# Adaptive-layernorm transformer block on eight cores: modulation vectors computed ahead of the layernorm, and the second gate folded into the down-projection weights

## What is computed

```python
mod = silu(c) @ wmod                         # [1, 6*2048] per core
sa, ca, ga, sb, cb, gb = split(mod, 6)
ga = (2*(ga >= 0) - 1) * maximum(abs(ga), 0.25)
gb = (2*(gb >= 0) - 1) * maximum(abs(gb), 0.25)
h = layernorm(x) * (1 + ca) + sa
x = x + ga * (attention(h, w_qkv) @ w_out)   # 16 heads of 128, no mask
h = layernorm(x) * (1 + cb) + sb
# router: silu(h @ r1.T) @ r2.T, the 16 best of 64 blocks of 128 hidden units
hidden = silu(h @ gate_w.T) * (h @ up_w.T) * block_mask
x = x + gb * (hidden @ down_w.T)
```

## Time and profile before

| | |
|---|---|
| median of 2 runs | 8536.75 us (8533.96 to 8539.55) |
| profiled execution | 8529.62 us |
| span of its slowest core (core 3) | 8527.7 us; the eight cores 8508.4 to 8527.7 |
| busy: TensorE, VectorE, ScalarE, GpSimd | 62%, 15%, 12%, 1% |
| mean granted TensorE clock, by core | 0.795 to 0.802 |
| HBM read / written by the core | 839.97 MB / 251.67 MB |

### The profile page before, as it was taken

One profiled execution on the slowest core, in us unless ns is written; L12 is line 12 of the kernel. 1 busy time (PEld: TensorE's weight loads), 2 busy tenths in 40 slices (PEclk: granted clock), 3 DMA queues, 4 the chain that ended last, 5 costly groups with the idle time before them and its releaser, 6 DMA issues.

```text
span 8527.7 us, 74717 instructions; the slowest of 8 cores (8508.4 to 8527.7 us)
## 1 busy us (share of the span) xinstructions
PE 5245.8 (62%) x25265; PEld 2424.2 (28%) x25265; DVE 1311.0 (15%) x2258; ACT 1063.2 (12%) x1243; POOL 81.8 (1%) x155
## 2 busy tenths in 40 slices
PE   4322002046666666666507888688885888958888
PEld 1101001023444434432203333233332333423333
DVE  2600000000000000010152210311203221031110
ACT  0100001023333333421110000000000000000000
POOL 1000000000000000000000000000000000000000
PEclk7555556578888888878758999799997999979999
DMA  7599999976666655200112334233342332412334
GB/s 130 112 118 115 112 111 111 110 121 126 130 128 130 131 131 143 54 12 20 39 58 90 104 103 132 73 102 104 104 138 65 103 104 100 148 60 99 104 114 134
DMA packets 1072418, 878.40 MB, mean 103 GB/s; under 512 B 782072, under 2 KB 962360, under 8 KB 1064768
## 3 DMA queue, kind: packets, MB, share of 16 engines
q1 hardware_dynamic: 908544, 605.16, 25.8%
q0 software_dynamic: 34096, 184.57, 17.9%
q10 hardware_dynamic: 129424, 83.91, 3.6%
HBM read 839.97 MB, written 251.67 MB: 128 GB/s over the span
## 4 chain that ended last, share of the span: by engine, by line
PE 56%; another core or an unknown queue 13%; DVE 11%; DMA 8%; issue 6%; ACT 6%; DVEq 1%; ACTq 0%; POOL 0%; POOLq 0%; SPq 0%
PE PS L925 13%; PE PS L978 10%; PE PS L932 10%; PE PS L580 6%; ACT A L614 5%; PE PS L687 3%; PE PS L628 3%; DMA R<-wmod 3%; PE PS L557 3%; DMA A<-wqkv_bf 2%; PE PS L605 2%; DVE R L949 2%; DVE dout_tile L944 2%; PE PS L888 1%
## 5 line engine op out<-in xcount | busy, mean ns | idle before, releaser
L580 PE MATMUL PS<-R,A 128*128 128x512 bf16 x2048 | 511.1, 416 | 1092.2 <-DMA A<-wqkv_bf 1092.2
L925 PE MATMUL PS<-A 128*128 128x512 bf16 x4096 | 1121.6, 436 | 3.0 <-DMA A<-wgT 2.9
L978 PE MATMUL PS<-R,A 128*128 128x512 bf16 x4096 | 915.4, 387 | 52.3 <-DMA A<-wdT 33.3
L932 PE MATMUL PS<-A 128*128 128x512 bf16 x4096 | 925.8, 379 | 0.0
L614 ACT ACTIVATE A<-PS,cexp 128x1024 bf16<-128x1024 f32 x512 | 616.7, 1204 | 435.3 <-PE PS L605 396.4
L925 PEld LDWEIGHTS PS<-A 128*128 128x128 bf16 x4096 | 428.1, 110 | 644.5 <-issue 333.5
L580 PEld LDWEIGHTS PS<-R,A 128*128 128x128 bf16 x2048 | 213.6, 105 | 1385.4 <-issue 1188.1
L605 PE MATMUL PS<-A 128*128 128x512 bf16 x1024 | 373.5, 473 | 376.0 <-ACT A L614 207.0
L978 PEld LDWEIGHTS PS<-R,A 128*128 128x128 bf16 x4096 | 405.4, 99 | 559.6 <-issue 98.7
L932 PEld LDWEIGHTS PS<-A 128*128 128x128 bf16 x4096 | 400.7, 98 | 483.4
L635 DVE RECIPROCAL inv<-PS 128x1 f32<-128x1 f32 x256 | 43.0, 168 | 2875.7 <-PE PS L628 2855.1
(11 more groups left out here) (121 smaller groups left out, 2135.1 us busy)
## 6 DMA issues: line engine op xcount, KB each, us to landing
A<-wgT SPq DMA_DIRECT2D x256, 512.0 KB, 3.7
A<-wuT SPq DMA_DIRECT2D x256, 512.0 KB, 4.6
A<-wdT SPq DMA_DIRECT2D x128, 1024.0 KB, 5.5
R<-wmod POOLq DMA_DIRECT2D x96, 512.0 KB, 6.6
wg_bf<-gate_w POOLq DMA_DIRECT2D x16, 2048.0 KB, 96.0
wd_bf<-down_w POOLq DMA_DIRECT2D x8, 4096.0 KB, 181.4
wu_bf<-up_w POOLq DMA_DIRECT2D x16, 2048.0 KB, 96.2
wgT<-A SPq DMA_DIRECT2D x64, 512.0 KB, 3.8
```

The lines of the kernel that those rows point to most:

```text
L580: e.matmul(o, l, r, start=s, stop=p), "pe")
L925: e.matmul(o, l, r, start=s, stop=p), "pe")
L932: e.matmul(o, l, r, start=s, stop=p), "pe")
L978: e.matmul(o, l, r, start=s, stop=p), "pe")
```

## The change

- **Modulation in one block, in smaller tiles.** `wmod` is read in 192 tiles of 2 x 128 x 512 (512 KB of f32, 256 KB of bf16) through a ring of six slots. Each group of 8 tiles fills one 512-column bank, which VectorE copies to `mod_raw`, on one partition. All 24 groups stand before the first layernorm group, on TensorE, VectorE and GpSimd alike. ScalarE's layernorm loads of `x` stand behind the forming of the gates, which needs all groups.
- **Gates** are formed from `mod_raw` in four pieces of 1024; `1 + cb` and `sb` are replicated right after.
- **Casts.** All of `w_qkv` and `w_out` follow the last `wmod` tile, then `gate_w` and `up_w`. The 8 casts of `down_w` are gone.
- **Fold.** In their place 256 steps: SyncE loads 128 x 512 of `down_w` in f32 (256 KB), VectorE multiplies by `gb_cols` into bf16, GpSimd stores it to `wd_bf` (128 KB). Two buffers each way. They stand on VectorE between the layernorm and the first attention head.
- **Preparation** waits for the last multiplication of the fold; its 192 steps are unchanged.
- **Down eviction** is a plain copy without the scale.

The diff, cut to its core:

```diff
+    wmod_ring = R2[:, 0:6144]
+    mod_raw = fv(A, 0, 12288, parts=1)
-    for idx in range(16):
-        mod_slab_dma(idx)
-        mod_slab_mms(idx)
-    t_bounce_pe = repl_from_banks(sa_repA, False, 0)
...
+    for nb_ in range(24):
+        bk = nb_ % 2
+        b.bank_acquire(bk)
+        for kcp in range(8):
+            slot = tile_idx % 6
+            if tile_idx >= 6:
+                b.wait("gp", "pe", mm_t[tile_idx - 6])
...
+            t_d = b.dma("gp", dst_ap, src_ap)
+            b.wait_tok("pe", t_d)
...
+            for sub in range(2):
...
+        t = b.op("dve", lambda e, d=mod_raw[0:1, nb_ * 512:(nb_ + 1) * 512],
+                 s=bank(bk)[0:1, :]: e.tensor_copy(d, s), "dve")
...
+        if nb_ == 7:
+            t_ca1 = replicate(mod_ca, ca1_repA, mod_evac[7], plus1=True)
+            t_sa = replicate(mod_sa, sa_repA, mod_evac[7])
...
-            for s2 in range(2):
-                mod_slab_dma(32 + 2 * i + s2)
-                mod_slab_mms(32 + 2 * i + s2)
...
+    b.wait_tok("dve", t_gbcols)
+    for k in range(256):
+        dc, part = k // 16, k % 16
+        pp = k % 2
+        if k >= 2:
+            b.wait("sp", "dve", wdf_ts_t[k - 2])
+        t_in = b.dma("sp", wdf_in[pp],
+                     wd_h[dc * 128:(dc + 1) * 128, part * 512:(part + 1) * 512])
+        b.wait_tok("dve", t_in)
+        if k >= 2:
+            b.wait_tok("dve", wdf_out_t[k - 2])
+        wdf_ts_t[k] = b.op("dve", lambda e, o=wdf_out[pp], i=wdf_in[pp],
+                           sc=gb_cols[:, dc:dc + 1]:
+                           e.tensor_scalar(o, i, sc, None, OP.mult), "dve")
+        b.wait("gp", "dve", wdf_ts_t[k])
+        wdf_out_t[k] = b.dma("gp", wd_bf[dc * 128:(dc + 1) * 128,
+                                         part * 512:(part + 1) * 512], wdf_out[pp])
...
+    b.wait("sp", "dve", wdf_ts_t[255])
...
-                            sc=gb_cols[:, dc:dc + 1]:
-                            e.activation(dout_tile, s, AF.Copy, scale=sc),
-                            "act")
+                    t_ev = b.op("act", lambda e, s=bank(bkd):
+                                e.activation(dout_tile, s, AF.Copy), "act")
```

More of the change, by code:

```diff
@@ L254, in build_nc @@
     ca1_repA = fv(A, 4096, 2048)
+    mod_sa = mod_raw[0:1, 0:2048]
+    mod_ca = mod_raw[0:1, 2048:4096]
+    mod_ga = mod_raw[0:1, 4096:6144]
+    mod_sbv = mod_raw[0:1, 6144:8192]
+    mod_cb = mod_raw[0:1, 8192:10240]
+    mod_gb = mod_raw[0:1, 10240:12288]
     b.op("dve", lambda e: e.memset(ones_f, 1.0), "dve")
@@ L277, in build_nc, with replicate @@
     t_siluc = b.op("act", lambda e: e.activation(silu_cb, c_sb, AF.Silu), "act")
[L279 to L323, removed]
+    def replicate(row_ap, dst_ap, dep_val, banks=(2, 3), plus1=False):
+        last = None
+        for j in range(4):
+            bk = banks[j % 2]
             b.bank_acquire(bk)
-            b.wait("pe", "dve", cp_t[q])
-            b.op("pe", lambda e, o=bank(bk), l=ones_f, r=bounce[q]:
+            b.wait("pe", "dve", dep_val)
+            b.op("pe", lambda e, o=bank(bk), l=ones_f,
+                 r=row_ap[0:1, j * 512:(j + 1) * 512]:
                  e.matmul(o, l, r, start=True, stop=True), "pe")
@@ L330, in repl_from_banks @@
             if plus1:
-                b.op("dve", lambda e, d=dst_ap[:, q * 512:(q + 1) * 512],
-                     s=bank(bk): e.tensor_scalar(d, s, 1.0, None, OP.add), "dve")
-            else:
-                b.op("dve", lambda e, d=dst_ap[:, q * 512:(q + 1) * 512],
-                     s=bank(bk): e.tensor_copy(d, s), "dve")
+                last = b.op("dve", lambda e, d=dst_ap[:, j * 512:(j + 1) * 512],
+                            s=bank(bk):
+                            e.tensor_scalar(d, s, 1.0, None, OP.add), "dve")
+            else:
+                last = b.op("dve", lambda e, d=dst_ap[:, j * 512:(j + 1) * 512],
+                            s=bank(bk): e.tensor_copy(d, s), "dve")
@@ L336, in repl_from_banks @@
             b.bank_read_done("dve", bk)
[L337 to L350, removed]
+        return last
@@ new lines, in build_nc @@
+    mm_t = {}
+    mod_evac = []
+    tile_idx = 0
+    for nb_ in range(24):
[5 more added lines that the diff above has]
+                b.wait("gp", "pe", mm_t[tile_idx - 6])
+            src_ap = wmod_h[2 * kcp * 128:(2 * kcp + 2) * 128,
+                            nb_ * 512:(nb_ + 1) * 512]
+            src_ap = src_ap.rearrange("(two p) j -> p two j", p=128)
+            dst_ap = wmod_ring[:, slot * 1024:(slot + 1) * 1024]
+            dst_ap = dst_ap.rearrange("p (two j) -> p two j", two=2)
+            t_d = b.dma("gp", dst_ap, src_ap)
+            b.wait_tok("pe", t_d)
+            if nb_ == 0 and kcp == 0:
+                b.wait("pe", "act", t_siluc)
+            for sub in range(2):
+                kc = 2 * kcp + sub
+                mm_t[tile_idx] = b.op(
+                    "pe", lambda e, o=bank(bk)[0:1, :],
+                    l=silu_cb[:, kc:kc + 1],
+                    r=wmod_ring[:, slot * 1024 + sub * 512:
+                                slot * 1024 + sub * 512 + 512],
+                    s=(kc == 0), p=(kc == 15):
+                    e.matmul(o, l, r, start=s, stop=p), "pe")
+            tile_idx += 1
+        b.bank_written(bk)
+        b.bank_read("dve", bk)
+        t = b.op("dve", lambda e, d=mod_raw[0:1, nb_ * 512:(nb_ + 1) * 512],
+                 s=bank(bk)[0:1, :]: e.tensor_copy(d, s), "dve")
+        b.bank_read_done("dve", bk)
+        mod_evac.append(t)
+        if nb_ == 7:
+            t_ca1 = replicate(mod_ca, ca1_repA, mod_evac[7], plus1=True)
+            t_sa = replicate(mod_sa, sa_repA, mod_evac[7])
@@ new lines, in build_nc @@
+    cast_order = [0, 2, 4, 1, 3, 5]
+    cast_qkv_t = [None] * 6
+    for ch in cast_order:
+        cast_qkv_t[ch] = b.dma("gp", wqkv_bf[:, ch * 1024:(ch + 1) * 1024],
+                               wqkv_h[:, ch * 1024:(ch + 1) * 1024])
+    cast_wout_t = [b.dma("gp", wout_bf[:, ch * 1024:(ch + 1) * 1024],
+                         wout_h[:, ch * 1024:(ch + 1) * 1024]) for ch in range(2)]
+    sgn_scr = fv(R2, 0, 1024)[0:1, :]
+    sgn2 = fv(R2, 2048, 1024)[0:1, :]
+    abs_scr = fv(R2, 4096, 1024)[0:1, :]
@@ L351, in gagb_post @@
+    abs2 = fv(R2, 6144, 1024)[0:1, :]
+    for row_base in (4096, 10240):
+        for hf in range(2):
+            seg = mod_raw[0:1, row_base + hf * 1024:row_base + (hf + 1) * 1024]
+            b.op("dve", lambda e, r=seg: e.tensor_scalar(
+                sgn_scr, r, 0.0, 2.0, OP.is_ge, OP.mult), "dve")
             b.op("dve", lambda e: e.tensor_scalar(
@@ L353, in gagb_post @@
             b.wait("act", "dve", b.cnt["dve"])
-            if q > 0:
-                b.wait_tok("act", toks[q - 1])
-            b.op("act", lambda e, s=src: e.activation(abs_scr, s, AF.Abs), "act")
+            b.op("act", lambda e, r=seg: e.activation(abs_scr, r, AF.Abs), "act")
             b.wait("dve", "act", b.cnt["act"])
[L358 to L366, removed]
-    for idx in range(16):
-        mod_slab_dma(idx)
-        mod_slab_mms(idx)
-    t_bounce_pe = repl_from_banks(sa_repA, False, 0)
[L372 to L376, removed]
+            b.op("dve", lambda e: e.tensor_scalar(abs2, abs_scr, 0.25, None, OP.max), "dve")
+            b.op("dve", lambda e, r=seg: e.tensor_mul(r, sgn2, abs2), "dve")
+    cb1_row = fv(R2, 0, 2048)[0:1, :]
+    t_modpost = b.op("dve", lambda e: e.tensor_scalar(cb1_row, mod_cb, 1.0, None, OP.add), "dve")
+    b.wait("act", "dve", t_modpost)
+    t1 = b.dma("sc", vec_scr[0:1, :], mod_ga)
+    t2 = b.dma("sc", vec_scr[1:2, :], mod_gb)
+    b.wait_tok("sp", t1)
+    b.wait_tok("sp", t2)
+    b.dma("sp", ga_cols, vec_scr[0:1, :].rearrange("a (k p) -> (a p) k", p=128),
+          slow_ok=True)
+    t_gbcols = b.dma("sp", gb_cols,
+                     vec_scr[1:2, :].rearrange("a (k p) -> (a p) k", p=128),
+                     slow_ok=True)
+    t_cb1 = replicate(cb1_row, cb1_rep, t_modpost)
+    t_sbr = replicate(mod_sbv, sb_rep, t_modpost)
     def ln_group_math(st, g):
@@ L461, in build_nc @@
[L461 to L486, removed]
@@ L488, in build_nc @@
-    cast_t = {}
[L489 to L497, removed]
+    cast_t = {}
@@ new lines, in build_nc @@
+    for name, src, dst in (("wg", wg_h, wg_bf), ("wu", wu_h, wu_bf)):
+        for ch in range(16):
+            cast_t[(name, ch)] = b.dma("gp", dst[ch * 512:(ch + 1) * 512, :],
+                                       src[ch * 512:(ch + 1) * 512, :])
+    b.wait_tok("dve", t_gbcols)
+    wdf_out_t = [0] * 256
+    wdf_ts_t = [0] * 256
+    for k in range(256):
[14 more added lines that the diff above has]
+                                         part * 512:(part + 1) * 512], wdf_out[pp])
@@ L504, in build_nc @@
     prep_wd_toks = []
[L505 to L522, removed]
-        prep_gu_toks.append(prep_last[0])
-        prep_t[name] = prep_last[0]
-    def wd_prep_step(cq):
-        if cq == 0:
```

(29 more changed lines are left out.)

30 lines of the change are left out of this document (3 added, 27 removed).

## The result

| | before | changed |
|---|---|---|
| median of all runs | 8832.54 us (10 runs) | 8995.54 us (11 runs) |
| lowest | 8533.96 | 8712.41 |
| profiled execution | 8529.62 | 8716.23 |
| spans of its eight cores | 8508 to 8528 | 8668 to 8715 |

The changed kernel is slower: the ratio is 1.0267, with an interval of 1.019 to 1.0343, so it is slower beyond the noise, but whether by more than 2% stays open. The profiled executions differ by 187 us, 2.2%. The forecast was 124 us.

What follows compares the result with a forecast made beforehand. Time is set by when attention runs freely, until now after the casts. Modulation 363, casts 1000, first step 6 and fold 486 give F = 1855; plus 112.8 minus 1843.7 is +124: 8654 us, range 8515 to 8900.

Steps and rivals of the forecast that it cites:

- modulation, end: `wmod` stage: 12 us start, 192 tiles at 1.78 us, 9 us for replications; 363 us, bounds 328 and 474.
- casts landed: Weight casts after modulation, without `down_w`: 1000 us, bounds 960 and 1050, last landed at 1363 us.
- a fold step: Fold behind the casts: half a two-buffer cycle of 3.8 us, 1.9 us; 256 steps 486 us, bounds 410 and 755.
- F to head 1's first division: Attention after the fold's end F: 51.8 us for three strips plus 61.0 us from even to odd head, 112.8 us.
- rival of short rows: Modulation: short rows slow a tile to 2.4 us, stage 474 us instead of 363, time 8765 us; chance 0.10.
- either arm: Fold buffer's cycle: load to multiplication's end, or multiplication to store's landing; each 3.2 us, giving at least 1.6 us a step.
- the term for the meeting: Fold: load and store meet at the DMA engines, 1.2 us of work per step; 0.6 us added to the cycle.
- The slow store: Rival, fold: GpSimd store lands only after 5 us, step 2.95, fold 755 us, time 8923 us; chance 0.25.
- The locked GpSimd: Rival, fold: each GpSimd issue waits out a VectorE multiplication, 105 us in all, time 8759 us; chance 0.04.
- The rule of the Trainium skill for small DMAs: Modulation tiles: one at a time, 192 would take about 615 us; not applied because five overlap.
- Preparation, layernorm, eviction: Preparation hidden by 320 us before attention's end; layernorm ends near 650 us, under the casts; plain down eviction gains nothing.

Runs made afterwards that it cites:

- e1: Changed kernel with the fold undone (`down_w` cast again, `gb` in the eviction), modulation block kept: 0.9959 of before, profiled 8508.3 us.
- e5: Changed kernel with all but the fold's first two loads left out: 1.71 us a step, stores land in 2.0 us.
- e6: Changed kernel without the fold's stores, `down_w` cast as before, multiplied tiles unused: 1.74 us a step, a load lands in 2.7 us.
- e8: Changed kernel with the fold in 64 steps of 128 x 2048, still two buffers each way: 8521.3 and 8527.6 us.
- e4: Changed kernel with five buffers each way in the fold instead of two: 8544.1 us, 1.33 us a step.
- e3: Changed kernel with the fold's stores issued by SyncE, ahead of the load: cores 0 to 3 8667 to 8704 us, against 8684 to 8696.

## Why the prediction was right or wrong

The mechanism was right (attention waits for the fold, and the fold for its two buffers), and one term of its sum was too small. By its steps, on the profiled core:

| step | forecast | measured |
|---|---|---|
| modulation, end | 363 us | 362 |
| casts landed | 1363 | 1348 |
| a fold step | 1.9 | 2.30 (2.12 to 2.31 by core) |
| fold | 486 | 584 |
| end of the fold, F | 1855 | 1933 |
| F to head 1's first division | 112.8 | 109.9 |
| head 1's first division, later by | 124 | 199 |
| time, profiled executions | +124 | +187 |

- **Modulation.** Right in kind and size: 150 GB/s written against 127, (359.1 - 5.3) / 192 = 1.84 us a tile with the replication, forecast 1.78 + 9 / 192 = 1.83. The rival of short rows at 2.4 us did not happen. That old and new stage differ by 300 us and the time by 14 is e1's answer.
- **Casts.** 986 us against 1000. The eight 4 MB pieces took about 47 us each beside the layernorm's loads; 336 + 50 was the forecast, 380 the measurement.
- **The fold: the step that failed.** I wrote a cycle of 3.2 us for either arm and added 0.6 for their meeting at the engines. Each arm alone is 3.4 to 3.5 (e5, e6), so the arms were well sized; the term for the meeting was not: with both arms a cycle is 4.6 us on core 6, so the meeting costs 1.1 to 1.2, and 0.8 on the core with the shortest fold. Most of it falls on the store: it lands in 2.0 us alone (e5) and in 3.2 with the loads (median), while a load goes from 2.7 (e6) to 3.0. The trace also shows what the 0.6 had left out. Evenly spaced, a cycle is 4.1 us, 0.7 above one arm, about as I forecast; in lockstep, which I had not thought of, both loads and both stores go out close together, a cycle is 4.95 us, and the meeting costs 1.5. Why the steps fall into lockstep is not shown. In the arm's sum there was luck: two of the smaller terms were low, 0.67 instead of 0.25 from VectorE to GpSimd's issue and 0.49 instead of 0.41 for a multiplication, and a shorter landing (2.0 for 2.4) hid this. Over the whole fold the 0.4 us a step is 98 us, more than the whole miss of 63; the casts, which ended 15 us early, and the 12 us below gave some of it back.
- **The slow store** was the rival nearest to the result: it put the 2% line at a step of 2.1 us, and the step is 2.30. But its reason, a store that takes 5 us by itself, is wrong; the median landing is 3.2 with the loads and 2.0 without.
- **The locked GpSimd.** In the cycle shown the issue starts 0.08 us after the second multiplication's end, which looks like the lock. It is not: where the steps are evenly spaced and no other multiplication runs (from 1801.35 to 1801.83, the issue at 1802.52), the issue is also 0.69 us behind its own multiplication. What a lock could explain is two issues of 0.74 and 0.72 us instead of 0.54, during which a multiplication started (at 1354.77 and 1363.69); the median of 256 is 0.539. The rule of the Trainium skill (SBUF — State Buffer, "Who interferes with whom") may show in these two; it cost next to nothing here.
- **The rule of the Trainium skill for small DMAs** (DMA: Bandwidth & Descriptors, "Bandwidth": batch to at least 1 MiB) was rightly set aside for the modulation, where five tiles overlap. In the fold, where only two steps overlap, following it pays: e8, with 1 MB loads, gets back some 190 us. But e4 gets back 172 with loads of 256 KB and five buffers, so size is one way and depth the other.
- **Preparation, layernorm, eviction** hid as said: 302 us between the preparation's last store and attention's end, forecast 320. The layernorm ended near 722 us, not 650, still long before F.
- **The 12 us between +199 at head 1 and +187** come from comparing two cores, the slowest of each kernel (3 before, 6 after): on core 6 alone head 1's first division is 203 us later and the span 205 us longer. Core for core the spans grew by 142 to 205 us, least on core 5, whose fold is the shortest, and most on core 6, whose fold is the longest. So with the fold of another core the same forecast would have missed by less.

What stays open: the executions behind the ratio range from 8712 to 8810 us for the changed kernel, while the three lowest of before lie within 7 us of each other, so the ratio (2.7%) is larger than the profiled pair's 2.2%. In the two longest the slowest core's granted clock is 0.780 and 0.782, where the profiled execution shows 0.790 on its own; how much of their time that is, no run says. Nor does one say why a core changes from lockstep to even spacing and back.

## What to carry to other kernels

Work that is folded into weights ahead of time is only free if the engine that does it is free at that place of its list: ask what stands behind it in program order, not how busy the engine is. A loop of load, compute and store through two buffers runs at latency; price it by one buffer's cycle with both transfers in flight, and with both buffers' transfers out together, and let depth or size grow until the DMA engines are full. And a stage made shorter in front of a queue of casts moves the time only as far as what follows the casts was waiting for them alone.

## What the hardware showed that was not expected

- From the end of a VectorE operation to the issue of a DMA that waits for it: 0.67 us on GpSimd, 0.12 to 0.14 on SyncE.
- A 128 KB store to HBM lands in 2.0 us whether GpSimd or SyncE issues it, and in 3.2 in the median when loads of 256 KB are issued just ahead of it on another queue (3.4 where two steps run in lockstep, 2.7 where they are evenly spaced).
- Beside casts in 32 KB rows a load of 256 KB in 2 KB rows lands 141 us after its issue in the median (e3, core 7), against 2.9 us without the casts; a step of one load and one store comes through every 70 us or so.
- The fold's 100 MB take about 340 us with five buffers or with large tiles, at a DMA share of 0.94 and 0.85; two small buffers leave nearly half of that unused.
